# Rearranged banks, gate steps and waits, and no full-array fillers in the main part of the self-attention

## The chip, the cores and the metric

One core of a Trainium2 chip runs the whole program. The time is the device time of one launch in microseconds; the median of several runs counts. TensorE multiplies (PE in the rows, its weight loads are PEld), VectorE is DVE, ScalarE is ACT, GpSimd is POOL, and SyncE (SP) issues the transfers.

## What is computed

A pre-norm decoder layer over x of 4 batches x 512 tokens x 128 features, in fp32: causal self-attention with one head, cross-attention with 16 heads to 154 context rows, a bidirectional self-attention with 16 heads and rotary positions, and a mixture of 8 experts with the two best of each token. The reference, cut and in its own names, with h(x) a LayerNorm:

```python
a = softmax(where(causal, (x@Wq)@(x@Wk).T / sqrt(128), -inf)) @ (x@Wv)      # front
o = softmax(where(mask == 0, -inf, q@k.T * scale)) @ v ; o @ wo + bo          # cross, 16 heads of 8
attn = softmax(rope(q)@rope(k).T / sqrt(HD)) @ v ; ao @ Wo + bo              # self, 16 heads of 8
gate_probs = softmax(x1 @ Wg + bg)
topk_p, topk_i = top_k(gate_probs, 2) ; topk_p /= sum(topk_p)
h = gelu(x1 @ W1 + b1) ; y = h @ W2 + b2                                      # 8 experts, 128 -> 512 -> 128
out = layernorm(x1 + sum_e comb[e] * y[e])
```

## The kernel before

The program is written by hand for each engine; every wait is on a counting semaphore, and each engine works through its own list in order. A batch n goes through `cross(n)`, `self_attention(n)` and `tail(n)`. TensorE writes into eight banks of 128x512 fp32.

*Experts.* The 32 chunks of a batch's experts (8 experts x 4 chunks of 128 hidden features; `up` makes the hidden rows, a gelu on ScalarE, `down` adds into bank 7) are spread over the gaps of the next batch, in an order written out in `MOE_GAPS`: so many chunks at each label, "x1" to "xq" in the cross-attention's scores, "w0" to "w6" after its sums, "ta" to "tf" in the tail. No chunk stands inside the self-attention. The last batch's chunks run in one piece at the end ("all"). One bank holds the hidden rows: `up(j)` waits for the gelu of chunk j-1 (`h_act`), line 1020. When an expert's four chunks are done, VectorE scales bank 7 by the gate weights (`scale_experts`, line 692) into `ys`, GpSimd adds that to `rT`, and the next expert's first `down` waits for the scaling.

*Gate.* VectorE finds the two best experts of each token in 16 small steps (`gate_step`, line 805 on), handed out between the row maxima of the next cross-attention (`GATE_STEPS`, line 858). Its step 3 waits for GpSimd's power e**(logit - max) (`gate_exp`, line 450), and GpSimd does the rstd of the finished batch's last LayerNorm before it. TensorE writes score banks ahead of VectorE's maxima, three pairs of banks at most.

*Cross-attention* (`cross`). Scores, row maxima on VectorE (line 867), then a second pass that computes the transposed scores with the maximum subtracted: the query stack in a bank (lines 1257, 1258: high and low parts by a selection matrix), minus the maxima (line 1263). Then exponentials, sums (lines 1273, 1275), all four groups into bank 3, each copied out to `ot` before the next; heads turned and normalised; output projection; LayerNorm `ln_rows(2)`, whose rstd is a power on GpSimd; projections and rotary positions.

*Self-attention* (`self_attention`). Four groups g of four heads. For each group and each of four blocks of 128 queries, four score matmuls `s1` (line 1345, 32 rows of the array each, so several run side by side) go to a ring of three banks, and VectorE takes their row maxima (line 936). The second pass of group g runs beside the maxima of group g+1: per step (g, c) one filler, `s2` of heads 0, 1 (line 1367), `s1`, `s2` of heads 2, 3, the value sums of the step before (`sums_of`, line 1377, 128 rows x 32 columns), `s1`. `q2` (lines 1352 to 1355) starts the next group when its maxima are done. In the last group there are no scores left, and the front of the next batch (its projections and causal scores, lines 1078 to 1094) stands there.

*Fillers.* `keep_warm(n, bank)` (line 1015) issues n matmuls of 128x128 by 128x512 whose result nobody reads. They stand three by three, or one by one beside the stacks, among the first group's scores, in the first batch wherever expert chunks would be, and one ahead of each step's `s2` in the main part:

```python
if i == 0:
    keep_warm(1, 4)
for q in range(2):
    hh = 2 * i + q
    ins = pe.matmul(bank[4 + hh], kst[blk(hh), g, c * P:(c + 1) * P], q2st[blk(hh), g, :], ...)
```

*End of a batch.* `end_rows` (lines 1168 to 1175) brings the experts' sum back to token rows: the gate weights times b2, plus `ys` of the last expert, plus `rT` of the seven before it. `end_step` is the last LayerNorm.

## Time and profile before

| | |
|---|---|
| median of 3 runs | 888.74 us (887.21 to 889.29) |
| the profiled execution | 887.32 us, span 885.5 us |
| mean granted TensorE clock | 0.961 of 2.4 GHz |
| busy: TensorE, VectorE, ScalarE, GpSimd | 791.1, 428.3, 358.9, 109.4 us |
| TensorE weight loads | 403.3 us (beside matmuls) |
| transfers | 19.94 MB, 7.1% of the 16 DMA engines' span in the main queue |

An engine's busy time is the union of its instructions; a row of TensorE's timeline that merges several instructions ends with the last one's drain, so the next row may start before it ends, and the spacing of starts is what an instruction costs there. An fp32 matmul shows as two records, one of the reduced fp32r format as one. PEclk is the granted share of 2.4 GHz: 1.00 or 0.50 (1.2 GHz), or a mean of both.

### The profile page before, as it was taken

Reading aid. Unit: us, or ns where it says so; the run is one execution under the profiler, and the core shown is the slowest. Engines: PE = TensorE matmul, PEld = TensorE weight load, DVE = VectorE, ACT = ScalarE, POOL = GpSimd, SP = SyncE. Lnnn points to the kernel's source line nnn. Section 1 sums busy time; section 2 is a strip of 40 time slices with the busy share of each in tenths; the row PEclk is TensorE's granted clock in tenths of the full one; section 3 lists DMA queues with packets and bytes.
Section 4 is the critical chain, followed back from the end, with each engine's and each line's share of the span. In section 5 each row is a group of like instructions: output and inputs, shape, how many; then the busy total and the mean of one; then the engine's idle time right before and its main releaser. Section 6 shows DMA issues by size and latency. Waiting matters only on the chain.

```text
span 885.5 us, 9314 instructions
## 1 busy us (share of the span) xinstructions
PE 791.1 (89%) x3541; PEld 403.3 (46%) x3549; DVE 428.3 (48%) x1021; ACT 358.9 (41%) x494; POOL 109.4 (12%) x84
## 2 busy tenths in 40 slices
PE   4999999997979999995998999995998999994995
PEld 2774644485533543554543444544543343441332
DVE  4473597456343685345524576444622588132002
ACT  1214147622533376640442377540342267621331
POOL 4100100012012000114002100023002100014111
PEclk9999999998999999997999999998898999996998
DMA  6600000000100000000100000000000000000110
GB/s 184 202 1 1 0 1 1 1 1 2 42 12 33 15 1 1 1 25 12 43 13 24 24 1 1 1 24 0 26 13 20 28 1 1 1 24 24 36 36 24
DMA packets 18213, 19.94 MB, mean 23 GB/s; under 512 B 1730, under 2 KB 11224, under 8 KB 18168
## 3 DMA queue, kind: packets, MB, share of 16 engines
q1 hardware_dynamic: 18168, 19.34, 7.1%
q8 instruction: 28, 0.46, 0.2%
q14 instruction: 17, 0.14, 0.1%
HBM read 18.22 MB, written 1.11 MB: 22 GB/s over the span
## 4 chain that ended last, share of the span: by engine, by line
PE 77%; DVE 9%; issue 6%; POOL 4%; ACT 2%; SPq 0%; DMA 0%; POOLq 0%; DVEq 0%; ACTq 0%
PE banks L1026 13%; PE banks L1037 11%; PE banks L1015 8%; PE banks L1377 7%; PE banks L1345 5%; PE banks L1367 3%; DVE nm L936 2%; POOL gt L450 2%; PE banks L1328 2%; PE banks L1275 2%; PE banks L1244 2%; PE banks L1273 2%; PE banks L1247 2%; PE banks L1292 1%; PE banks L1286 1%
## 5 line engine op out<-in xcount | busy, mean ns | idle before, releaser
L504 ACT ACTIVATE hT<-banks,cols 128x512 f32<-128x512 f32 x128 | 87.9, 687 | 243.4 <-PE banks L1026 243.2
L936 DVE TENSOR_REDUCE nm<-banks 128x1 fp32r<-128x512 f32 x256 | 161.3, 685 | 32.4 <-PE banks L1345 31.2
L1026 PE MATMUL banks<-x1T,w 128*128 128x512 f32 x256 | 144.8, 648 | 2.4 <-ACT hT L504 2.4
L1037 PE MATMUL banks<-hT,w 128*128 128x512 f32 x256 | 134.9, 611 | 11.0 <-DVE ys L692 11.0
L635 ACT ACTIVATE px<-banks 128x1024 f32<-128x1024 f32 x128 | 125.5, 1023 | 45.3 <-PE banks L1367 44.9
L1015 PE MATMUL banks<-sel_r,eye_r 128*128 128x512 f32 x304 | 101.6, 433 | 1.0 <-ACT px L635 0.9
L692 DVE TENSOR_TENSOR ys<-banks,combB 128x512 f32<-128x512 f32 x32 | 22.1, 690 | 149.5 <-PE banks L1037 149.5
L1037 PEld LDWEIGHTS banks<-hT,w 128*128 128x128 f32 x256 | 47.7, 194 | 78.3 <-issue 51.5
L417 POOL TENSOR_TENSOR rstd<-ve,misc 128x4 f32<-128x4 f32 x20 | 20.3, 1016 | 452.0 <-DVE ve L673 452.0
L1026 PEld LDWEIGHTS banks<-x1T,w 128*128 128x128 f32 x256 | 41.8, 196 | 66.1 <-ACT hT L504 58.4
L1377 PE MATMUL banks<-px,vf 128*32 128x512 f32 x512 | 69.1, 612 | 1.4 <-ACT px L635 0.7
L1015 PEld LDWEIGHTS banks<-sel_r,eye_r 128*128 128x128 f32 x304 | 55.1, 190 | 31.6 <-issue 17.2
L1345 PE MATMUL banks<-kst,qst 32*128 32x512 f32 x256 | 66.5, 470 | 0.0
L1345 PEld LDWEIGHTS banks<-kst,qst 32*128 32x128 f32 x256 | 31.6, 182 | 52.7 <-DVE nm L936 35.6
L432 POOL TENSOR_TENSOR rT<-rT,ys 128x512 f32<-128x512 f32 x24 | 31.5, 1314 | 194.5 <-DVE ys L692 194.5
L1367 PE MATMUL banks<-q2st,kst 32*128 32x512 f32 x256 | 55.6, 500 | 0.0
L867 DVE TENSOR_REDUCE nm<-banks 128x4 fp32r<-128x616 f32 x64 | 48.7, 794 | 11.6 <-PE banks L1247 11.6
L1244 PE MATMUL banks<-mb,eye_b 128*128 128x308 bf16 x128 | 31.0, 327 | 25.6 <-DVE nm L867 24.8
L591 ACT ACTIVATE px<-banks 128x1024 f32<-128x1024 f32 x32 | 31.5, 1022 | 21.9 <-PE banks L1292 21.6
L1247 PE MATMUL banks<-kbd,qst 128*128 128x308 f32 x128 | 38.6, 386 | 0.0
L895 DVE COPY ot<-banks 128x512 f32<-128x512 f32 x16 | 11.1, 692 | 54.2 <-PE banks L1275 54.2
L1367 PEld LDWEIGHTS banks<-q2st,kst 32*128 32x128 f32 x256 | 21.8, 183 | 20.0 <-issue 17.3
(230 smaller groups left out, 947.4 us busy)
## 6 DMA issues: line engine op xcount, KB each, us to landing
combB<-gate_weights SPq DMA_DIRECT2D x32, 256.0 KB, 3.0
w<-in_L_ffn_W SPq DMA_DIRECT2D x1, 2048.0 KB, 9.5
msk<-in_mask SPq DMA_DIRECT2D x4, 308.0 KB, 4.0
xin<-in_x SPq DMA_DIRECT2D x4, 256.0 KB, 4.2
ot<-in_const_sel SPq DMA_DIRECT2D x1, 1024.0 KB
out<-outb SPq DMA_DIRECT2D x4, 256.0 KB, 2.3
cos<-in_const_cos SPq DMA_DIRECT2D x1, 256.0 KB
sin<-in_const_sin SPq DMA_DIRECT2D x1, 256.0 KB
```

Of the source, the lines that this page charges most:

```text
L504: act.activation(hT[:, j % 2, :], bank[H_BANK], ACT.Gelu, bias=cols[:, ROW_B1 + j:ROW_B1 + j + 1]).then_inc(k["h_act"], 1)
L635: act.activation(px[:, c % 2, 2 * i:2 * i + 2, :], banks[:, 4 + 2 * i:6 + 2 * i, :], ACT.Exp, scale=SCALE_H).then_inc(k["f_exp"], 1)
L867: dve.tensor_reduce(nm[:, t, g, :].rearrange("p (b h c) -> p b h c", b=2, h=2)[:, :, :, 0], banks[:, a:a + 2, 0:2 * KC].rearrange("p b (h ...
L936: dve.tensor_reduce(nm[:, t, g, BLK * hh:BLK * hh + 1], bank[s1_bank(g, t, hh)], AX.X, ALU.max, negate=True).then_inc(k["f_max"], 1)
L1015: pe.matmul(bank[i], eye_r[:], sel_r[:, 0].rearrange("p g q -> p (g q)"), start=True, stop=True)
L1026: pe.matmul(bank[H_BANK], w1[:, e, c * P:(c + 1) * P], x1T[:, p % 2, :], start=True, stop=True).then_inc(k["h_ready"], 1)
L1037: pe.matmul(bank[Y_BANK], w2[:, FC * e + c, :], hT[:, j % 2, :], start=(c == 0), stop=(c == FC - 1)).then_inc(k["y_part"], 1)
L1244: pe.matmul(bank[i][:, 0:2 * KC], eye_b[:], mb[:, t, :].unsqueeze(1).to_broadcast([P, 2, KC]), start=True, stop=False, skip_group_check=True)
L1247: ins = pe.matmul(bank[i][:, 0:2 * KC], qst[:, g, t * P:(t + 1) * P], kbd[:, g, 2 * h:2 * h + 2, :], start=False, stop=True, skip_group_ch ...
L1345: pe.matmul(bank[s1_bank(g, t, hh)], qst[blk(hh), g, t * P:(t + 1) * P], kst[blk(hh), g, :], start=True, stop=True).then_inc(k["f_s1"], 1)
L1367: ins = pe.matmul(bank[4 + hh], kst[blk(hh), g, c * P:(c + 1) * P], q2st[blk(hh), g, :], start=True, stop=True)
L1377: ins = pe.matmul(bank[3][blk(hh), :], vf[:, c, HG * g + hh, :], px[:, c % 2, hh, :], start=(c == 0), stop=(c == T - 1), skip_group_check= ...
```

## The change

What the diff does, part by part:

- A second bank (5) for the hidden rows from chunk 4 of a batch on; `up(j)` then waits for gelu j-2 only. To free bank 5 in the gaps, the uses of banks 0 to 5 in `tail`, `cross` and the first stacks are renumbered, with waits for the former users.
- The gate compares logits, not probabilities. The power takes the difference of the two best (4 values a partition instead of 32), at step 8, and its result is used at step 12. At the end of the program GpSimd does this power ahead of the second last batch's rstd, and VectorE does steps 1 to 8 ahead of that batch's moments.
- After the cross-attention the scaling of gap "w3" stands ahead of `ln_rows(2)`.
- The last group's sum of the cross-attention goes to bank 0 and waits for no copy.
- `q2` and its sibling in the cross-attention take the query stack from `qst` by one matmul with the identity.
- `end_rows` of batches 0 to 2 takes all eight experts from `rT` (GpSimd adds the eighth too) and drops the four matmuls over `ys`.
- `turn_heads` of blocks 2 and 3 both stand behind `a_sums`.
- The filler ahead of `s2` is issued only in the last group of the last batch. All other fillers stay.

```diff
@@ -105,7 +105,8 @@
-H_BANK, Y_BANK = 6, 7
+H_BANKS, Y_BANK = (6, 5), 7
+SINGLE_BANK = 4
@@ -115,7 +116,7 @@
-ST_BANKS = (4, 5, 6, 7, 4, 5, 6, 7)
+ST_BANKS = (3, 4, 5, 6, 7, 4, 5, 6)
@@ -147,6 +148,11 @@
+
+
+def h_bank(j):
+
+    return H_BANKS[0] if j < SINGLE_BANK else H_BANKS[j % 2]
@@ -307,8 +313,10 @@
-        XQ_BANKS = (0, 1, 4, 5)
+        XQ_BANKS = (1, 2, 4, 5)
...
+        X_SUM_BANKS = (3, 3, 3, 0)
+        X_HEAD_BANKS = (4, 1, 2, 3)
@@ -428,7 +436,7 @@
-                        pool.wait_ge(k["rT_added"], (NE - 1) * p + e)
+                        pool.wait_ge(k["rT_added"], NE * p + e)
@@ -447,7 +455,7 @@
-                pool.tensor_tensor(gt[:, 1], euler[:], gt[:, 0], ALU.pow).then_inc(k["g_exp"], 1)
+                pool.tensor_tensor(gs[:, 6, :], euler[:], gs[:, 5, :], ALU.pow).then_inc(k["g_exp"], 1)
@@ -483,8 +491,8 @@
                 tail(n)
+            gate_exp(B - 1)
             rstd_of(4, B - 2)
-            gate_exp(B - 1)
             end(B - 2)
@@ -685,10 +693,8 @@
                     dve.wait_ge(k["comb_loaded"], 16 * (NE * p + e + 1))
-                    if e:
-                        dve.wait_ge(k["rT_added"], (NE - 1) * p + e)
-                    elif p:
-                        dve.wait_ge(k["r_turned"], p)
+                    if p or e:
+                        dve.wait_ge(k["rT_added"], NE * p + e)
                     dve.tensor_tensor(ys[:], bank[Y_BANK], combB[:], ALU.mult).then_inc(k["y_scaled"], 1)
@@ -732,8 +738,7 @@
                     normalise_heads(0, p, 1, 4)
-                    normalise_heads(1, p, 1, 5)
-                    normalise_heads(2, p, 1, 3)
+                    normalise_heads(1, p, 1, 3)
                 if ahead:
@@ -742,7 +747,8 @@
-                    normalise_heads(3, p, 1, 4)
+                    normalise_heads(2, p, 1, 4)
+                    normalise_heads(3, p, 1, 3)
@@ -808,40 +814,40 @@
-                    own.inc(dve.reduce_max(gs[:, 0, :], flat(2), AX.X))
+                    own.inc(dve.reduce_max(gs[:, 1, :], flat(2), AX.X))
...
-                    dve.tensor_tensor(flat(0), flat(2), per_token(0), ALU.subtract).then_inc(k["g_shift"], 1)
+                    own.inc(dve.tensor_tensor(flat(3), flat(2), per_token(1), ALU.is_equal))
...
+                    own.inc(dve.tensor_tensor(flat(5), flat(3), rank, ALU.mult))
+                elif i == 4:
+                    own.inc(dve.reduce_max(gs[:, 2, :], flat(5), AX.X))
+                elif i == 5:
+                    own.inc(dve.tensor_tensor(flat(4), flat(5), per_token(2), ALU.is_equal))
+                elif i == 6:
+                    own.inc(dve.scalar_tensor_tensor(flat(8), flat(4), NEG, flat(2), ALU.mult, ALU.add))
+                elif i == 7:
+                    own.inc(dve.reduce_max(gs[:, 3, :], flat(8), AX.X))
+                elif i == 8:
+                    dve.tensor_tensor(gs[:, 5, :], gs[:, 3, :], gs[:, 1, :], ALU.subtract).then_inc(k["g_shift"], 1)
+                    own.inc(dve.tensor_tensor(flat(6), flat(8), per_token(3), ALU.is_equal))
+                elif i == 9:
+                    own.inc(dve.tensor_tensor(flat(9), flat(6), rank, ALU.mult))
+                elif i == 10:
+                    own.inc(dve.reduce_max(gs[:, 4, :], flat(9), AX.X))
+                elif i == 11:
+                    own.inc(dve.tensor_tensor(flat(7), flat(9), per_token(4), ALU.is_equal))
+                elif i == 12:
...
-                    own.inc(dve.reduce_max(gs[:, 1, :], flat(1), AX.X))
-                elif i == 4:
-                    own.inc(dve.tensor_tensor(flat(3), flat(1), per_token(1), ALU.is_equal))
-                elif i == 5:
-                    own.inc(dve.tensor_tensor(flat(5), flat(3), rank, ALU.mult))
-                elif i == 6:
-                    own.inc(dve.reduce_max(gs[:, 2, :], flat(5), AX.X))
-                elif i == 7:
-                    own.inc(dve.tensor_tensor(flat(4), flat(5), per_token(2), ALU.is_equal))
-                elif i == 8:
-                    own.inc(dve.scalar_tensor_tensor(flat(8), flat(4), -4.0, flat(1), ALU.mult, ALU.add))
-                elif i == 9:
-                    own.inc(dve.reduce_max(gs[:, 3, :], flat(8), AX.X))
-                elif i == 10:
-                    own.inc(dve.tensor_tensor(flat(6), flat(8), per_token(3), ALU.is_equal))
-                elif i == 11:
-                    own.inc(dve.tensor_tensor(flat(9), flat(6), rank, ALU.mult))
-                elif i == 12:
-                    own.inc(dve.reduce_max(gs[:, 4, :], flat(9), AX.X))
+                    own.inc(dve.tensor_scalar(gs[:, 0, :], gs[:, 6, :], 1.0, None, ALU.add))
...
-                    own.inc(dve.tensor_tensor(flat(7), flat(9), per_token(4), ALU.is_equal))
+                    own.inc(dve.reciprocal(gs[:, 7, :], gs[:, 0, :]))
...
-                    own.inc(dve.tensor_tensor(flat(2), flat(4), flat(7), ALU.add))
-                    own.inc(dve.tensor_tensor(gs[:, 5, :], gs[:, 1, :], gs[:, 3, :], ALU.add))
+                    own.inc(dve.tensor_tensor(gs[:, 8, :], gs[:, 6, :], gs[:, 7, :], ALU.mult))
+                    own.inc(dve.tensor_tensor(flat(0), flat(4), per_token(7), ALU.mult))
...
-                    own.inc(dve.tensor_tensor(flat(3), flat(2), flat(1), ALU.mult))
-                    own.inc(dve.reciprocal(gs[:, 6, :], gs[:, 5, :]))
+                    own.inc(dve.tensor_tensor(flat(1), flat(7), per_token(8), ALU.mult))
...
-                    dve.tensor_tensor(comb[:], flat(3), per_token(6), ALU.mult).then_inc(k["g_comb"], 1)
+                    dve.tensor_tensor(comb[:], flat(0), flat(1), ALU.add).then_inc(k["g_comb"], 1)
@@ -855,7 +861,7 @@
-            GATE_STEPS = ((1, 2), (3,), (4,), (5, 6), (7,), (8, 9), (10,), (11, 12), (13, 14), (15, 16))
+            GATE_STEPS = ((1,), (2, 3), (4, 5), (6,), (7, 8), (9, 10), (11,), (12, 13), (14,), (15, 16))
@@ -892,30 +898,30 @@
-                    dve.tensor_copy(ot[:, g, :], bank[3]).then_inc(k["x_ot"], 1)
+                    dve.tensor_copy(ot[:, g, :], bank[X_SUM_BANKS[g]]).then_inc(k["x_ot"], 1)
...
-                    normalise_heads(t, n, 0, (4, 5, 0, 1)[t])
+                    normalise_heads(t, n, 0, X_HEAD_BANKS[t])
...
-                own.inc(dve.tensor_tensor(x2[:].rearrange("p t d -> p (t d)"), bank[3],
+                own.inc(dve.tensor_tensor(x2[:].rearrange("p t d -> p (t d)"), bank[4],
...
+                scale_experts(p, "w3")
...
-                scale_experts(p, "w3")
...
-                    dve.scalar_tensor_tensor(rope_t[:, 2 * i, :], bank[2 * i], cols[:, ROW_FBQ + i:ROW_FBQ + i + 1],
+                    dve.scalar_tensor_tensor(rope_t[:, 2 * i, :], bank[1 + 2 * i], cols[:, ROW_FBQ + i:ROW_FBQ + i + 1],
...
-                    dve.scalar_tensor_tensor(rope_t[:, 2 * i + 1, :], bank[2 * i + 1], cols[:, COL_FBQR + i:COL_FBQR + i + 1],
+                    dve.scalar_tensor_tensor(rope_t[:, 2 * i + 1, :], bank[2 + 2 * i], cols[:, COL_FBQR + i:COL_FBQR + i + 1],
@@ -988,11 +994,11 @@
-            gate_step(B - 1, 1)
-            gate_step(B - 1, 2)
+            for i in range(1, 9):
+                gate_step(B - 1, i)
...
-            for i in range(3, 17):
+            for i in range(9, 17):
@@ -1017,13 +1023,13 @@
-                    pe.wait_ge(k["h_act"], NJ * p + j)
+                    pe.wait_ge(k["h_act"], NJ * p + (j if j <= SINGLE_BANK else j - 1))
...
-                pe.matmul(bank[H_BANK], w1[:, e, c * P:(c + 1) * P], x1T[:, p % 2, :], start=True,
+                pe.matmul(bank[h_bank(j)], w1[:, e, c * P:(c + 1) * P], x1T[:, p % 2, :], start=True,
@@ -1133,15 +1139,16 @@
+                pe.wait_ge(k["a_done"], n + 1)
+                pe.wait_ge(k["mT_ready"], 2 * (n + 1))
...
-                    dst = bank[4 + g // 2][:, (g % 2) * KC:(g % 2 + 1) * KC]
+                    dst = bank[1 + g // 2][:, (g % 2) * KC:(g % 2 + 1) * KC]
...
-                pe.wait_ge(k["x_v"], (1 + HG) * (n + 1))
@@ -1163,17 +1170,27 @@
-                pe.wait_ge(k["y_scaled"], NE * (p + 1))
-                for t in range(T):
-                    pe.matmul(bank[Y_BANK][:, t * P:(t + 1) * P], combT[:, t * P:(t + 1) * P], b2[:], start=(t == 0),
-                              stop=False, skip_group_check=True)
-                for t in range(T):
-                    pe.matmul(bank[Y_BANK][:, t * P:(t + 1) * P], ys[:, t * P:(t + 1) * P], eye[:], start=False,
-                              stop=False, skip_group_check=True)
-                pe.wait_ge(k["rT_added"], (NE - 1) * (p + 1))
-                for t in range(T):
-                    ins = pe.matmul(bank[Y_BANK][:, t * P:(t + 1) * P], rT[:, t * P:(t + 1) * P], eye[:], start=False,
-                                    stop=True, skip_group_check=True)
+                tokens = lambda t: slice(t * P, (t + 1) * P)
+                if p < B - 1:
+                    pe.wait_ge(k["rT_added"], NE * (p + 1))
+                    for t in range(T):
+                        pe.matmul(bank[Y_BANK][:, tokens(t)], rT[:, tokens(t)], eye[:], start=(t == 0),
+                                  stop=False, skip_group_check=True)
+                    for t in range(T):
+                        ins = pe.matmul(bank[Y_BANK][:, tokens(t)], combT[:, tokens(t)], b2[:], start=False,
+                                        stop=True, skip_group_check=True)
+                else:
+                    pe.wait_ge(k["y_scaled"], NE * (p + 1))
+                    for t in range(T):
+                        pe.matmul(bank[Y_BANK][:, tokens(t)], combT[:, tokens(t)], b2[:], start=(t == 0),
+                                  stop=False, skip_group_check=True)
+                    for t in range(T):
+                        pe.matmul(bank[Y_BANK][:, tokens(t)], ys[:, tokens(t)], eye[:], start=False,
+                                  stop=False, skip_group_check=True)
+                    pe.wait_ge(k["rT_added"], NE * (p + 1) - 1)
+                    for t in range(T):
+                        ins = pe.matmul(bank[Y_BANK][:, tokens(t)], rT[:, tokens(t)], eye[:], start=False,
+                                        stop=True, skip_group_check=True)
@@ -1188,17 +1205,18 @@
-                    turn_heads(1, 5)
-                    turn_heads(2, 3)
+                    turn_heads(1, 3)
...
-                    turn_heads(3, 4)
+                    turn_heads(2, 4)
+                    pe.wait_ge(k["on_ready"], T * (2 * p + 1) + 2)
+                    turn_heads(3, 3)
...
-                    pe.wait_ge(k["on_ready"], T * (2 * p + 1) + 2)
-                    turn_normalised(p, 1, 5)
+                    pe.wait_ge(k["on_ready"], T * (2 * p + 1) + 3)
+                    turn_normalised(p, 1, 4)
@@ -1209,12 +1227,12 @@
-                    turn_rows(1, n, hat1, 1)
+                    turn_rows(1, n, hat1, 4)
...
-                    pe.wait_ge(k["mT_ready"], 2 * (n + 1))
-                    pe.matmul(bank[2], wx[:, 0, :], hatT[:], start=True, stop=True).then_inc(k["x_qproj"], 1)
+                    pe.wait_ge(k["x_v"], (1 + HG) * (n + 1))
+                    pe.matmul(bank[0], wx[:, 0, :], hatT[:], start=True, stop=True).then_inc(k["x_qproj"], 1)
@@ -1253,9 +1271,7 @@
-                    dst = bank[XQ2_BANKS[g]]
-                    pe.matmul(dst, sel_r[:, 0, g, :], qhi[:], start=True, stop=False, skip_group_check=True)
-                    pe.matmul(dst, sel_r[:, 1, g, :], qlo[:], start=False, stop=False, skip_group_check=True)
+                    pe.matmul(bank[XQ2_BANKS[g]], eye_r[:], qst[:, g, :], start=True, stop=False, skip_group_check=True)
@@ -1267,12 +1283,13 @@
-                    if g:
+                    acc = bank[X_SUM_BANKS[g]]
+                    if 0 < g < G - 1:
...
-                        pe.matmul(bank[3][blk(hh), :], vx[:, HG * g + hh, :], px[:, g % 2, hh, :], start=True,
+                        pe.matmul(acc[blk(hh), :], vx[:, HG * g + hh, :], px[:, g % 2, hh, :], start=True,
...
-                    pe.matmul(bank[3], vxt[:, g, :], pxt[:, g % 2, :], start=False, stop=True,
+                    pe.matmul(acc, vxt[:, g, :], pxt[:, g % 2, :], start=False, stop=True,
@@ -1349,8 +1366,7 @@
-                    pe.matmul(dst, sel_r[:, 0, g, :], qhi[:], start=True, stop=False, skip_group_check=True)
-                    pe.matmul(dst, sel_r[:, 1, g, :], qlo[:], start=False, stop=False, skip_group_check=True)
+                    pe.matmul(dst, eye_r[:], qst[:, g, :], start=True, stop=False, skip_group_check=True)
@@ -1360,7 +1376,7 @@
-                    if i == 0:
+                    if i == 0 and g == G - 1 and b == B - 1:
@@ -1385,9 +1401,8 @@
-                            if t == 1 and i == 0 and b:
+                            if t == 2 and i == 0 and b:
...
-                                pe.wait_ge(k["h_act"], NJ * (b - 1) + FC * EXPERTS_BEFORE_F)
@@ -1401,7 +1416,7 @@
-                pe.wait_ge(k["f_st"], (2 * G - 1) * b + 5)
+                pe.wait_ge(k["f_st"], (2 * G - 1) * b + 6)
```

## Rows read from the trace of the kernel before

**Rows 1.** The page, chain that ended last: share of the span by engine.
```profile
PE 77%; DVE 9%; issue 6%; POOL 4%; ACT 2%; SPq 0%; DMA 0%; POOLq 0%; DVEq 0%; ACTq 0%
```

**Rows 2.** Waits: who waited for whom; us in total, times, longest.
```profile
DVE gs L816 <- POOL gt L450: 22.5, 4, 7.0
PE banks L1161 <- DVE comb L844: 13.6, 1, 13.6
PE banks L1037 <- DVE ys L692: 11.0, 3, 3.7
```

**Rows 3.** Timeline, gate: start us, us, instruction, idle before and releaser.
```profile
406.43 1.02 POOL L417 TENSOR_TENSOR rstd<-ve,misc 128x4 f32<-128x4 f32 x1 [16.55 <-DVE ve L673]
...
407.42 5.43 POOL L450 TENSOR_TENSOR gt<-euler,gt 128x32 f32<-128x32 f32 x1
...
804.49 0.19 DVE L816 TENSOR_REDUCE gs<-gt 128x4 f32<-128x32 f32 x1 [4.04 <-POOL gt L450]
```

**Rows 4.** Timeline, TensorE and VectorE, output part of the third batch's cross-attention.
```profile
463.63 1.02 PE L1026 MATMUL banks<-x1T,w 128*128 128x512 f32 x2
...
464.49 1.02 PE L1037 MATMUL banks<-hT,w 128*128 128x512 f32 x2
...
467.53 2.05 DVE L679 TENSOR_SCALAR hat<-x,mean,rstd 128x128 f32<-128x128 f32 x4 [1.13 <-POOL rstd L417]
469.50 0.68 DVE L692 TENSOR_TENSOR ys<-banks,combB 128x512 f32<-128x512 f32 x1
470.23 1.17 PE L1037 MATMUL banks<-hT,w 128*128 128x512 f32 x2 [3.67 <-DVE ys L692]
...
476.33 0.60 PE L1055 MATMUL banks<-eye,hat 128*128 128x128 f32 x4
```

**Rows 5.** Timeline, TensorE, the closing run of experts.
```profile
816.60 1.13 PE L1026 MATMUL banks<-x1T,w 128*128 128x512 f32 x2
...
817.56 1.02 PE L1037 MATMUL banks<-hT,w 128*128 128x512 f32 x2
...
818.50 1.13 PE L1026 MATMUL banks<-x1T,w 128*128 128x512 f32 x2
```

**Rows 6.** Timeline, TensorE: end rows, and the last sum of a cross-attention.
```profile
400.19 1.16 PE L1171 MATMUL banks<-eye,ys 128*128 128x128 f32 x8
...
451.54 1.06 PE L1273 MATMUL banks<-px,vx 128*32 128x512 f32 x8 [0.88 <-DVE ot L895]
```

**Rows 7.** Timeline, second group of the third batch's self-attention, TensorE and VectorE.
```profile
529.19 0.50 PE L1367 MATMUL banks<-q2st,kst 32*128 32x512 f32 x2
...
529.62 1.06 PE L1377 MATMUL banks<-px,vf 128*32 128x512 f32 x8
...
530.61 0.50 PE L1345 MATMUL banks<-kst,qst 32*128 32x512 f32 x2
...
531.04 0.50 PE L1015 MATMUL banks<-sel_r,eye_r 128*128 128x512 f32 x1
531.14 2.48 DVE L936 TENSOR_REDUCE nm<-banks 128x1 fp32r<-128x512 f32 x4 [0.22 <-PE banks L1345]
...
531.89 0.50 PE L1367 MATMUL banks<-q2st,kst 32*128 32x512 f32 x2
```

**Rows 8.** Timeline, TensorE, the stacks of the second pass.
```profile
523.06 0.39 PE L1353 MATMUL banks<-qlo,sel_r 128*128 128x512 f32 x1
523.29 0.56 PE L1355 MATMUL banks<-eye_r,nm 128*128 128x128 f32 x4
```

**Rows 9.** Stretches: us, busy (instructions) of PE, PEld, DVE, ACT, POOL, PEclk, DMA.
```profile
341.85:361.77 19.92, 19.23 (x108) 7.75 (x109) 6.83 (x15) 12.34 (x20) 0.00 (x0) 0.91 0.00 1
546.40:564.95 18.55, 17.85 (x108) 7.54 (x109) 6.83 (x15) 12.29 (x20) 0.00 (x0) 1.00 0.00 0
...
341.50:344.90 3.40, 2.79 (x17) 1.61 (x19) 1.79 (x4) 1.94 (x3) 0.00 (x0) 1.00 0.00 0
344.90:348.30 3.40, 3.40 (x17) 0.78 (x13) 0.00 (x0) 1.26 (x3) 0.00 (x0) 0.50 0.00 0
```

**Rows 10.** Timeline, TensorE, at the low clock.
```profile
344.73 1.84 PE L1377 MATMUL banks<-px,vf 128*32 128x512 f32 x8
...
346.50 0.80 PE L1015 MATMUL banks<-sel_r,eye_r 128*128 128x512 f32 x1
```

36 lines of the change are left out of this document (18 added, 18 removed).

## Prediction

> **What bounds the kernel now.** I read the chain of waits first: TensorE carries 77% of it [rows 1]. So a microsecond counts where TensorE runs without a gap, or where TensorE itself stands. The table of waits then gives the stops that lie on that chain. VectorE waits 22.5 us in four pieces for GpSimd's exponential of the gate, TensorE waits 13.6 us once for the last batch's gate weights, and 11.0 us in three pieces for the scaled expert output [rows 2]. The timeline shows why: the gate's power over 32 elements takes 5.43 us on GpSimd and stands behind a rstd of 1.02 us [rows 3], and in the output part TensorE stands 3.67 us for the scaling, which VectorE does behind the four normalised rows (467.53, 2.05 us), which wait for a rstd [rows 4]. In the self-attention the question is another one: is it TensorE that is full, filler included, or a loop through VectorE beside which the filler lies [rows 7]? Last comes the granted clock by stretch [rows 9].
>
> **The change, part by part.** The sum is made against the profiled execution's own 887.3 us (span 885.5), which lies 1.4 us under the median of the runs.
>
> Gate. The power moves from step 2 to step 8 and works on 4 elements a partition instead of 32, so it should cost about what a rstd of 128x4 costs, 1.02 instead of 5.43 us [rows 3]. Its result is asked for four steps later (step 12), with two row maxima between; I cost it at nothing, its cover being those maxima. If that cover were too short, about 1 us a batch would come back. The steps stay 18 small operations. The fourth of the four stops is the one in the end phase, 4.0 us [rows 3], so the three cross-attentions lose 22.5 - 4.0 = 18.5 us of VectorE stop, and TensorE stands behind VectorE there. TensorE comes out of the two longer stops at the low clock; I add half a microsecond: **19**. In the end phase the order also puts eight gate steps and the small power ahead of the LayerNorm's rows. Of the 13.6 us wait [rows 2] the 4.0 go, and part of the wait for the rstd is covered: **4.3** (4.0 to 5.5).
>
> Scaling ahead of the rows. From the first expert matmul after the output projection to the transposes of the rows are 476.33 - 463.63 = 12.70 us [rows 4]. In it stand four chunks, 8 matmuls of 0.86 us (464.49 - 463.63, the spacing where nothing waits [rows 4]), so 6.9 us. The scaling no longer waits for the rstd (1.02 us [rows 3]) and for the four rows (2.05 us); TensorE then waits about 1.0 us instead of 3.67. The rows are ready before TensorE asks. New length 7.9, gain 4.8, three times: **14.4** (3 x 2.7 = 8 if only the wait shrinks). Nothing new queues behind the scaling but the rows themselves, 0.7 us later, under four chunks of matmuls.
>
> Two hidden banks. An up and a down matmul take 1.90 us a chunk now (818.50 - 816.60 [rows 5]), since the up waits for the gelu of the chunk before. With the second bank the up needs no gelu, and a chunk takes 2 x 0.86 = 1.72. The down that opens an expert still waits for the scaled output, so three chunks of four gain 0.19. In the closing run of 28 chunks past the single-bank ones that is 21 x 0.19 = 4.0. In the gaps about 9 chunks of a batch follow one another: 27 x 0.19 = 5.1, less where another engine ends the stage, 4.5. Together **8.5** (5 to 11).
>
> Small parts. The query stacks of the second pass take one matmul instead of two, 0.23 us [rows 8]: 4 x 4 in the cross-attention are 3.7; in the self-attention 16, of which those behind the first maxima give part of it to the wait for one more stack copy: 3.4. The last sum of the cross-attention no longer waits 0.88 us for a copy out of its bank [rows 6]: 3.5. The rows of the finished batch lose the eight records over ys, about 1.0 us of the 1.16 shown [rows 6], in two batches; in the third they wait for GpSimd's last addition instead (1.3 us of work against 1.0 saved), so 0: 2.0. Sum **12.6**. The moved head transposes, the renumbered banks and the other new waits are for things long done; 0, up to 0.5 us each if a copy is late.
>
> Fillers. In the steady part one step is 2.70 us (531.89 - 529.19). Follow the loop: the second-pass pair starts at 529.19 together with the last score matmul before it, the value sums at 529.62, the next score pair at 530.61; VectorE begins its four maxima at 531.14 (2.48 us, 0.62 each), and when the first is done and its bank free, the next score matmul and second-pass pair start, 531.89 [rows 7]. 0.43 + 0.99 + 0.53 + 0.75 = 2.70: the loop closes without the filler, which stands at 531.04 beside VectorE's first maximum. So its 0.43 us (the mode change, as from 529.19 to 529.62) are worth **0** in the 36 steps that have maxima beside them (upper end: VectorE's gap of 0.22 in each [rows 7], 8 us). In the fourth group the maxima are over and TensorE does the next batch's front: there up to 4 x 0.43 a batch in three batches; the exponentials end part of it, so 1.3 each: **3.8**.
>
> Sum: 19 + 4.3 + 14.4 + 8.5 + 12.6 + 3.8 = 62.6 us of gain, 824.7.
>
> Now the clock. The filler does a second thing: it is work. In the second batch the granted clock fell from 2.4 to 1.2 GHz at 344.9 although the fillers are there; in the 3.40 us before, TensorE was busy 2.79, so it stood 0.61 in all [rows 9]. The other batches went through the same place at the full clock. The margin is thin with fillers and thinner without. One fall costs what that batch lost against the next: 19.92 - 18.55 = 1.37 us [rows 9]. I take one or two falls a batch, five more than now: **-7** (0 to -16). 824.7 + 7 = 831.7; forecast **832 us**.
>
> The Trainium skill, "TensorE: Matmul & The Clock Gate", states under "HAM oscillation" that gaps between matmuls must be long for the clock to drop; by that nothing falls here and the result would be 825. Its next section, "A second HAM failure mode: psum-queue depth-cycling", says that short micro-idles between groups of matmuls are enough to make the clock oscillate. The fall at 344.9 with no long gap before it [rows 9] speaks for the second, and what it would do here is rival 2. "TensorEngine Tiling (Array Packing)", "Key Properties", has it that a change of tiling mode drains the array; a lone filler's 0.43 us against 0.23 for one in a row [rows 7, 8] agrees, and a TensorE that was the bound would gain that much a step.
>
> **Rivals.**
> 1. *The fillers were on the path.* If VectorE's gap of 0.22 us is TensorE's doing, 36 steps gain 8 us more: 824. For it: TensorE is without a gap in the steady part. Against it: the loop closes without the filler, though the two paths lie within some 0.1 us of each other. Chance 0.15.
> 2. *The clock falls and is slow to return.* At 1.2 GHz a value-sum group takes 346.50 - 344.73 = 1.77 us instead of 0.99, and a lone filler lasts 0.80 instead of 0.50 [rows 7, 10]; a step becomes about 4.0 instead of 2.7, 1.3 more. If the low clock holds a good third of the 48 steps, 16 x 1.3 = 21, and as much again in the front matmuls and transitions: 865. For it: at half the clock the same work fills more of the time, which speaks for a quick return, but each return can be followed by a fall. Chance 0.17.
> 3. *Slower than before*, by the same mechanism when it decides: low through the whole self-attention, 12 steps x 1.3 = 16, the front and the transitions some 12, the first pass some 8, so 36 us a batch and about 140 in four: 965 in full, and over 889 once the low clock holds over 62.6/140 = 45% of the self-attention. Chance 0.04; when it falls at all, the fp32 front work of each batch should bring it back.
> 4. *The stop only moves:* VectorE waits for the small power, or GpSimd's additions come late. 3 to 5 us in all, inside the forecast's range; no case of its own.
>
> **How the numbers follow.** Forecast 0.61 (822 to 845), fillers on the path 0.15 (816 to 826), slow return 0.17 (845 to 885), slower 0.04, something I have not seen 0.03. Range 816 to 858: it holds the first two and a third of the third. A measurement of this kernel tells 0.2%, some 2 us, from no change. Faster by over that 0.95, within 0.01, slower 0.04.
>
> **What would show it.** The gate's power near 1.0 us, no stop of VectorE before its sum, and cross-attentions of the last three batches shorter by 5 to 8 us each. No 3.7 us wait of TensorE for ys, and 4.8 us less between the two points of [rows 4]. A chunk of the closing run at 1.72, 1.90 at each expert's start. Steps of the self-attention still at 2.70 with VectorE's gap still there; if they are at 2.5, rival 1. Granted clock: a handful of short falls between the groups; long stretches at 1.2 GHz would be rival 2 or 3. I am wrong if the steps lengthen at the full clock, or if the stops mended on one engine come back as waits on another.

## The result, and the profile after

| | before | after |
|---|---|---|
| median of 4 runs | 889.01 us (887.21 to 889.38) | 865.50 us (854.96 to 867.45) |
| the profiled execution | 887.32 us, span 885.5 us | 867.45 us, span 865.6 us |
| mean granted TensorE clock | 0.961 | 0.910 |

Ratio 0.972 (0.964 to 0.980): 23.5 us faster, where the forecast said 57. The executions of the changed kernel lie 12.5 us apart and those of the kernel before 2.2. Below, medians and ranges are of all executions of a kernel, since that spread is part of what is explained, and ratios only of those within 1.5% of its fastest.

The page of the changed kernel, the chain that ended last, and the granted clock in 40 slices of the span:

```profile
PE 80%; DVE 13%; issue 3%; ACT 2%; POOL 1%; SPq 0%; DMA 0%; POOLq 0%; DVEq 0%; ACTq 0%
...
PEclk9899999999999986998999955998999965895998
```

GpSimd's 4% of the chain [rows 1] are down to 1%. The clock has three dips of two or more slices with a 5 or 6 in them; the first, at the slices 15 and 16, begins at 317.5 us.

The waits that answer to [rows 2] (who waited for whom; total us, times, longest):

```profile
PE banks L1168 <- DVE comb L850: 9.6, 1, 9.6
...
PE banks L1043 <- DVE ys L698: 2.1, 3, 0.7
```

VectorE's wait for the gate's power, 22.5 us before, has no row any more, and the waits for the scaled output are 2.1 instead of 11.0 us. The stops were mended. So where did the 33.5 us over the forecast's 832 go? The main part of the self-attention, from the first value sums to the last, as stretches (length, busy time with instruction counts of PE, PEld, DVE, ACT, POOL, then PEclk), four batches of the kernel before:

```profile
127.94:175.21 47.27, 46.19 (x281) 19.15 (x282) 29.86 (x52) 32.60 (x41) 0.00 (x0) 1.00 0.00 1
312.51:361.18 48.67, 47.60 (x283) 19.36 (x282) 29.85 (x52) 32.92 (x41) 0.00 (x0) 0.96 0.01 1
517.09:564.36 47.27, 46.19 (x283) 19.15 (x282) 29.85 (x52) 32.86 (x41) 0.00 (x0) 1.00 0.00 1
721.99:765.33 43.34, 41.49 (x255) 16.02 (x254) 24.79 (x40) 32.37 (x37) 0.00 (x0) 1.00 0.00 1
```

and of the changed kernel:

```profile
128.14:173.87 45.73, 39.63 (x265) 14.91 (x265) 29.87 (x52) 33.06 (x41) 0.00 (x0) 1.00 0.00 1
298.17:352.05 53.88, 48.19 (x265) 16.58 (x265) 29.61 (x52) 33.75 (x41) 0.00 (x0) 0.78 0.00 1
491.86:552.91 61.05, 55.97 (x265) 18.56 (x265) 29.61 (x52) 34.10 (x41) 0.00 (x0) 0.64 0.00 1
692.95:750.10 57.15, 51.20 (x241) 15.95 (x241) 24.45 (x40) 33.34 (x37) 0.00 (x0) 0.64 0.00 1
```

The first batch keeps the full clock and is 1.54 us shorter than before. The other three have mean clocks of 0.78, 0.64 and 0.64, so 24, 44 and 41 us at 1.2 GHz (twice what is missing to 1, times the length). Against 45.7 us at the full clock they lose 8.2 and 15.3. The last batch has no front behind it and would take 42.2 at the full clock by an estimate (42.3 and 42.6 in two runs below, with fillers), so it loses 15.0. Together: **38.4 us**. Without the falls this execution would have taken some 829.

What the fall looks like, third batch, first the stretches on either side of it, then of the rise:

```profile
495.10:498.50 3.40, 2.78 (x19) 1.45 (x13) 3.16 (x6) 1.72 (x3) 0.00 (x0) 0.98 0.00 0
498.50:501.90 3.40, 3.40 (x15) 0.71 (x13) 0.35 (x1) 1.74 (x3) 0.00 (x0) 0.50 0.00 0
...
505.30:508.70 3.40, 3.05 (x16) 0.58 (x12) 2.48 (x4) 2.37 (x3) 0.00 (x0) 0.50 0.00 0
...
539.40:542.80 3.40, 3.40 (x20) 1.07 (x16) 0.69 (x1) 2.29 (x3) 0.00 (x0) 0.51 0.00 0
542.80:546.20 3.40, 3.40 (x22) 1.08 (x24) 1.14 (x3) 1.96 (x3) 0.00 (x0) 1.00 0.02 5
```

No long wait stands ahead of the fall; TensorE was busy 2.78 of 3.40 us, its longest wait 0.43. Once the clock is low, TensorE is busier than that, 3.05 to 3.40 us of each 3.40 but for one piece with a wait of 1.47 at the end of group 3, and yet the clock stays low for 44 us. It rises at 542.75, in group 4, where no scores are left and TensorE has no wait for VectorE's maxima:

```profile
534.34 0.77 PE L1369 MATMUL banks<-qst,eye_r 128*128 128x512 f32 x1 [1.47 <-DVE nm L942]
...
540.96 1.12 PE L1061 MATMUL banks<-eye,hat 128*128 128x128 f32 x4
...
542.74 1.06 PE L1393 MATMUL banks<-px,vf 128*32 128x512 f32 x8
543.73 1.98 PE L1084 MATMUL banks<-hatT,wa 128*128 128x512 f32 x4
```

Of the next batch's front, only four small transposes (L1061) stand ahead of the rise; its projections come 1 us after. In the last batch, which has no front, the clock rises at 740.73, in group 4 too, behind the first of the fillers that stayed there.

A step at the full clock (first batch) and a step at the low one (third batch), TensorE and VectorE:

```profile
149.54 0.50 PE L1383 MATMUL banks<-q2st,kst 32*128 32x512 f32 x2
149.97 1.07 PE L1393 MATMUL banks<-px,vf 128*32 128x512 f32 x8
...
150.97 0.50 PE L1362 MATMUL banks<-kst,qst 32*128 32x512 f32 x2
...
151.50 2.48 DVE L942 TENSOR_REDUCE nm<-banks 128x1 fp32r<-128x512 f32 x4 [0.23 <-PE banks L1362]
...
152.25 0.50 PE L1362 MATMUL banks<-kst,qst 32*128 32x512 f32 x1 [0.43 <-DVE nm L942]
...
521.15 0.79 PE L1383 MATMUL banks<-q2st,kst 32*128 32x512 f32 x2
521.87 1.94 PE L1393 MATMUL banks<-px,vf 128*32 128x512 f32 x8
...
525.31 0.79 PE L1362 MATMUL banks<-kst,qst 32*128 32x512 f32 x1 [0.35 <-DVE nm L942]
```

At the full clock a step is 152.25 - 149.54 = 2.71 us without its filler, 2.70 with it [rows 7]: the filler's place is now a wait of 0.43 for VectorE. At the low clock it is 525.31 - 521.15 = 4.16.

### The profile page after: what moved, and what is told of

Read it like the earlier page. It is cut to its first block, busy times and chain, and to the rows that moved or that the text cites. A ratio compares the mean times of both kernels' runs of the same rounds, so it can differ in the third digit from the quotient of the medians.

```text
span 865.6 us, 9085 instructions
## 1 busy us (share of the span) xinstructions
PE 785.1 (91%) x3425; PEld 393.3 (45%) x3433; DVE 432.0 (50%) x1021; ACT 363.0 (42%) x494; POOL 95.5 (11%) x87
## 4 chain that ended last, share of the span: by engine, by line
PE 80%; DVE 13%; issue 3%; ACT 2%; POOL 1%; SPq 0%; DMA 0%; POOLq 0%; DVEq 0%; ACTq 0%
PE banks L1032 12%; PE banks L1043 12%; PE banks L1393 10%; PE banks L1362 7%; PE banks L1021 6%; DVE nm L942 5%; PE banks L1383 2%; PE banks L1345 2%; PE banks L1292 2%; PE banks L1290 2%; PE banks L1262 2%; PE banks L1066 2%; PE banks L1265 2%; PE banks L1309 1%; DVE nm L873 1%
## 5 line engine op out<-in xcount | busy, mean ns | idle before, releaser
L1032 PE MATMUL banks<-x1T,w 128*128 128x512 f32 x256 | 135.4, 611 | 0.8 <-ACT hT L512 0.8
L1362 PE MATMUL banks<-kst,qst 32*128 32x512 f32 x256 | 88.8, 557 | 14.8 <-DVE nm L942 14.8
L1393 PE MATMUL banks<-px,vf 128*32 128x512 f32 x512 | 89.8, 782 | 1.4 <-ACT px L643 0.7
L1362 PEld LDWEIGHTS banks<-kst,qst 32*128 32x128 f32 x256 | 35.5, 214 | 101.5 <-DVE nm L942 84.9
L1043 PEld LDWEIGHTS banks<-hT,w 128*128 128x128 f32 x256 | 46.8, 191 | 71.6 <-issue 49.4
L1383 PE MATMUL banks<-q2st,kst 32*128 32x512 f32 x256 | 70.6, 607 | 2.1 <-ACT px L643 1.2
L1021 PE MATMUL banks<-sel_r,eye_r 128*128 128x512 f32 x244 | 71.7, 417 | 0.1
L1032 PEld LDWEIGHTS banks<-x1T,w 128*128 128x128 f32 x256 | 46.8, 195 | 44.4 <-issue 39.1
L440 POOL TENSOR_TENSOR rT<-rT,ys 128x512 f32<-128x512 f32 x27 | 35.4, 1311 | 215.3 <-DVE ys L698 215.3
L873 DVE TENSOR_REDUCE nm<-banks 128x4 fp32r<-128x616 f32 x64 | 48.6, 794 | 10.1 <-PE banks L1265 10.1
L1021 PEld LDWEIGHTS banks<-sel_r,eye_r 128*128 128x128 f32 x244 | 44.0, 191 | 17.1 <-issue 7.0
L1383 PEld LDWEIGHTS banks<-q2st,kst 32*128 32x128 f32 x256 | 26.1, 219 | 17.0 <-issue 7.6
```

The costliest lines, as they stand in the source:

```text
L873: dve.tensor_reduce(nm[:, t, g, :].rearrange("p (b h c) -> p b h c", b=2, h=2)[:, :, :, 0], banks[:, a:a + 2, 0:2 * KC].rearrange("p b (h ...
L1021: pe.matmul(bank[i], eye_r[:], sel_r[:, 0].rearrange("p g q -> p (g q)"), start=True, stop=True)
L1032: pe.matmul(bank[h_bank(j)], w1[:, e, c * P:(c + 1) * P], x1T[:, p % 2, :], start=True, stop=True).then_inc(k["h_ready"], 1)
L1043: pe.matmul(bank[Y_BANK], w2[:, FC * e + c, :], hT[:, j % 2, :], start=(c == 0), stop=(c == FC - 1)).then_inc(k["y_part"], 1)
L1362: pe.matmul(bank[s1_bank(g, t, hh)], qst[blk(hh), g, t * P:(t + 1) * P], kst[blk(hh), g, :], start=True, stop=True).then_inc(k["f_s1"], 1)
L1393: ins = pe.matmul(bank[3][blk(hh), :], vf[:, c, HG * g + hh, :], px[:, c % 2, hh, :], start=(c == 0), stop=(c == T - 1), skip_group_check= ...
```

## The experiments

"Three groups" below means one filler a step in groups 1 to 3 of each batch and in group 4 of the last batch.

**Mended stops alone.** In the changed kernel:

```diff
-                    if i == 0 and g == G - 1 and b == B - 1:
+                    if i == 0:
                         keep_warm(1, 4)
```

> The changed kernel with the full-array filler back in every step of the self-attention, so the mended stops alone. In the changed kernel the stretches outside the self-attention loop lost 51.2 us against the kernel before, and the loop of the first batch, at the full clock all through, lost 1.6; the loops of the other three gained 5.2, 13.8 and 13.8 us, with TensorE at 1.2 GHz in most of them. Theory A (the missing fillers let the clock fall): with fillers the loops are back at 12.3 us a group of four steps, 0.2 under before for the shorter query stack, and the kernel takes 887.3 - 51.2 - 2.4 = 833.7, say 829 to 838. Theory B (the mended stops themselves, one matmul instead of two in the query stacks, let the clock fall, fillers or not): low stretches of 24 to 44 us stay in batches 2 to 4, 855 to 868.

838.21 us (832.88 to 844.66), ratio to before 0.942 (0.935 to 0.950), at the upper end of theory A's range. Its four loops (the main parts of the self-attention) took 46.6, 50.7, 46.6 and 44.1 us, with 10.2 us at 1.2 GHz in the second and 3.4 in the last. That is theory A in the main. But the kernel before, with its fillers in the same places, has 3.4 us in all, and six of its seven executions beside these lie within 2.5 us of each other. That the mended stops add some falls of their own, a part of theory B, is not ruled out.

**Fillers taken out, nothing mended.** The opposite edit in the kernel before.

> The kernel before with its fillers taken out of the self-attention loop except in the last group of the last batch, nothing mended. Theory A: the loops of the last three batches go to some 54 to 61 us as in the changed kernel, 37.4 us more than they would take at the full clock, against 0.9 us a batch that the last group gains: 889 + 34 = 923 (905 to 930). Theory B: the clock falls only with the mended stops, so this one is 885 to 889. A third, that falls depend on where the self-attention starts: some batches low and others not, 895 to 915.

907.44 us (907.07 to 921.46), ratio 1.020 (1.016 to 1.025). In the profiled execution (921.46) the loops of the first and third batch took 59.6 and 65.3 us and those of the others 47.5 and 44.4. So the missing fillers cost 18 us by themselves in the median, half of what I expected, and in that execution the first batch fell. Some loops low and others not, at 907 us, is also what the third expectation had. In the first batch the clock came back at 167.24, in the third group, where neither a filler nor a front matmul stands.

**Three groups.** `if i == 0 and (g < G - 1 or b == B - 1)`.

> The mended stops with the filler in groups 1 to 3 of every batch and in group 4 of the last batch alone. Theory A: the first batch showed group 4 and the end of group 3 0.9 us shorter without fillers at the full clock; the next batch's front matmuls are full-array work of their own there. So 833.7 - 3 x 0.9 = 831, 827 to 836, and no low stretch longer than 7 us in the loop. If the filler in group 4 is needed too, a low stretch begins in group 4 of some batch and the time is 835 to 845.

835.00 us (827.16 to 838.97), ratio 0.938 (0.931 to 0.945). Three loops at the full clock, 45.7, 45.7 and (last batch) 42.6; the third 54.3, with one low stretch of 24 us. So one filler a step makes a fall rarer but doesn't rule it out, and it doesn't end one at once either: the 24 us passed with a filler in each step. The time is not told apart from that of the run with fillers in every group.

**A filler of 32 rows,** in the same places:

```diff
-                        keep_warm(1, 4)
+                        pe.matmul(bank[4], kst[blk(0), g, 0:P], qst[blk(0), g, :], start=True, stop=True)
```

> As the run with fillers in three groups, but each filler is a matmul of the kind of the scores: 32 rows of the array, 128 columns, 512 columns of data in f32, which takes TensorE as long (0.43 us). Theory A1 (what counts is that the whole array works, not that TensorE is busy): the clock falls as without fillers, 860 to 872. Theory A2 (any work in the gap counts): as with full-array fillers, 827 to 838.

864.33 us (860.47 to 871.36), ratio 0.973 (0.967 to 0.979): no help, loops of 59.9, 59.9, 53.8 and 42.3 us. But the traces show that such a filler runs beside the scores. One group at the full clock, first with the 32-row filler, then with one full-array filler a step:

```profile
510.00:522.32 12.32, 10.87 (x77) 4.19 (x73) 9.74 (x17) 9.46 (x12) 0.00 (x0) 1.00 0.00 0
```

```profile
128.98:141.27 12.29, 11.87 (x73) 4.92 (x73) 9.77 (x17) 8.52 (x11) 0.00 (x0) 1.00 0.00 1
```

TensorE is busy 10.87 us against 11.87, so this run alone doesn't say whether the array or the time was missing. Three later runs take that up.

**Every other step,** of the three groups (`c % 2 == 0`).

> As the run with fillers in three groups (835.0 us), but in every other step only. Theory A (full-array work is what holds the clock, and each filler adds to it): the clock is lost in some of the batches, for a part of the loop, 843 to 858, between 835 with a filler in each step and 865 with none. If one filler in two steps suffices: 827 to 839. If one in two is as good as none: 860 to 870.

848.42 us (845.13 to 853.79), ratio 0.955 (0.951 to 0.959): half the fillers, half the gain.

**Two a step,** `keep_warm(2, 4)`, three groups.

> As the run with fillers in three groups, but two in a row in each step. The run with one a step still had one low stretch of 24 us in the third batch's loop, worth 54.3 - 45.7 = 8.6 us. Theory A: with twice the full-array work no long low stretch is left in any loop, and the second filler, without a change of mode, costs 0.2 us at most where it has no cover: loops of 45.7 to 48, kernel 825 to 834, and the spread of its runs smaller. Rival: the second filler stands on the path, 12 steps x 4 x 0.21 = 10 us: groups of 13.1 instead of 12.3, kernel 836 to 845.

831.18 us (829.78 to 832.27), ratio 0.935 (0.933 to 0.937). The loops took 46.0, 46.0, 46.0 and 43.5 us and the spread is down to 2.5 us. A group:

```profile
313.24:325.68 12.44, 12.30 (x81) 4.93 (x85) 10.31 (x16) 8.83 (x11) 0.00 (x0) 1.00 0.01 1
```

12.44 instead of 12.30: the second filler costs 0.14 us a group, not the 0.84 of the rival, and no loop has a fall. Against the undisturbed loops with one filler a step, these are 0.3 us longer, the last one 0.9, and the stretch from a batch's first scores to its first value sums is 0.24 longer, some 2.8 us in all. The fastest execution with one a step, 827.16 us, is below all of these.

**The changed kernel, 2 us later.** `keep_warm(10, 6)` ahead of the first tail.

> The changed kernel as it is, with ten full-array matmuls (2.1 us) put ahead of everything that follows the set-up, so that all later work comes some 2 us later. In the changed kernel the first batch's loop stayed at the full clock and the other three fell, with the same work in each. Theory C (without fillers each loop stands at the edge, and whether it falls, and where, is a matter of when it starts): other batches or other points of the loops fall, loops of 46 to 62 us in another pattern, 855 to 875. Rival (the first batch stays up because of something in it, such as its missing expert chunks): the same three batches fall in the same groups, and the first stays at 45.7.

860.48 us, from 841.07 to 885.39. In the profiled execution the loops took 48.1, 46.6, 52.8 and 56.7 us, where they took 45.7, 53.9, 61.1 and 57.2 before the shift. All four had a fall, of 6.8, 3.4, 20.5 and 41.0 us. The rival, that something in the first batch protects it, falls. The third one ended, at 529.21, ahead of the first front matmul (L1061), in the middle of a row of value sums, which take 1.94 us at the low clock and 1.06 at the full one:

```profile
526.23 1.94 PE L1393 MATMUL banks<-px,vf 128*32 128x512 f32 x8
...
528.83 1.23 PE L1393 MATMUL banks<-px,vf 128*32 128x512 f32 x8
529.99 0.66 PE L1061 MATMUL banks<-eye,hat 128*128 128x128 f32 x4
```

So the front's full-array work isn't needed for the rise. That the moment of the start alone decides isn't shown, since the executions of this one program differ by 44 us.

**Is it time or the array?** Two 32-row fillers ahead of each step's second-pass scores; then a third ahead of the other pair; then one filler a step from the same buffers on all 128 rows (`kst[:, g, 0:P]`, `qst[:, g, :]`).

> The changed kernel with two fillers of 32 rows in a row ahead of each step's second-pass scores (groups 1 to 3, and group 4 of the last batch). One such filler gave 864.3 us and TensorE busy 10.87 of 12.32 us in a group at the full clock. With two I expect 11.5 to 12.3 busy. If time in which TensorE works is what the missing fillers took away: 828 to 845. If it is work of the whole array: low stretches of 20 to 45 us in at least two of the four loops, 855 to 880.

838.61 us (837.10 to 854.88); TensorE busy 11.65 of 12.30 us in a group; loops 49.4, 46.9, 45.7 and 48.3. The time is in the range of the theory that counts time, though two loops had a low stretch of 10 and 17 us.

> As the run before it with a third filler of 32 rows, ahead of the step's other pair of second-pass scores. TensorE should have no idle time left, 12.3 of 12.5 us or more in a group as with two full-array fillers (831.2 us); the third stands on the path for 0.2 to 0.4 us a step, up to 15 us in the kernel. If time is what counts: no long low stretch, 832 to 848. If the whole array's work is: low stretches as without fillers, 865 to 900.

889.68 us (856.96 to 897.07). A group at the full clock, and the stretch ahead of a fall in the second batch:

```profile
300.90:314.12 13.22, 12.64 (x81) 5.36 (x81) 9.99 (x17) 9.80 (x11) 0.00 (x0) 1.00 0.00 1
...
317.70:321.10 3.40, 3.12 (x23) 1.80 (x16) 2.95 (x5) 1.70 (x3) 0.00 (x0) 1.00 0.00 0
321.10:324.50 3.40, 3.40 (x16) 1.03 (x15) 0.06 (x2) 1.48 (x2) 0.00 (x0) 0.51 0.02 5
```

> As the run with one filler of 32 rows a step, with the same operands on all 128 rows: one two-pass matmul of 128x128 by 128x512, 0.43 us at the full clock and some 0.4 more for the two changes of mode around it. Either theory expects the clock held: 827 to 840; if it stands on the path with 0.2 us a step, groups of 13.1 and 836 to 845. At 855 or more neither theory would be right, and it would be the reduced format of the fillers that matters.

839.02 us (832.97 to 842.87), with the pattern of the three-groups run: 45.7, 45.7, 54.4 and 42.7. The expectation calls its filler a two-pass matmul, but the buffers `kst` and `qst` hold the reduced format, and it is one record a step in the trace, as the other fillers are:

```profile
133.57 0.49 PE L1380 MATMUL banks<-qst,kst 128*128 128x512 f32 x1
```

With three small fillers TensorE is busy 12.64 of 13.22 us, about the share that one full-array filler a step gives (11.87 of 12.29). The longer steps explain some 0.92 x 3 x 4 = 11 us over the 831 without falls, and the executions lie 15 to 55 us above that, against 0 to 12 for the one full-array filler over its lowest. So filling TensorE's time isn't enough. All fillers, small and large, are of the reduced format, so it doesn't tell them apart; whether it matters, no run shows. Two small fillers did better than three, which neither theory expected.

How long the clock was at 1.2 GHz within the four loops, one trace a kernel:

| fillers ahead of `s2` | us at 1.2 GHz |
|---|---|
| none | 109 (changed kernel), 72 (2 us later), 99 (kernel before) |
| a full-array one in every other step of three groups | 72 |
| a full-array one a step | 3.4 (kernel before) and 14 (changed kernel), in every group; 24, 24 and 14, in three groups |
| two full-array ones a step | 0 in all five traces |
| 32 rows: one, two, three a step | 106, 30, 51 |

That full-array fillers keep the clock up, and two a step better than one, is shown. Whether they do it because the whole array works or because TensorE has fewer pauses stays open: two small ones did nearly as well as one large one, three did worse.

**The terms of the sum, one at a time.** Both on the version with two fillers a step, whose clock is steady. The rows ahead of the scaling again:

```diff
-                scale_experts(p, "w3")
                 ln_rows(2, n, x2, hat3, k["ln_hat2"])
+                scale_experts(p, "w3")
```

> As the run with two fillers a step (831.2 us), but VectorE again does the four normalised rows ahead of the scaling in the output part, as in the kernel before: this sizes one term of the forecast by itself. The forecast had 4.8 us a batch for it, 14.4 in three, from 12.70 us to 7.9 between the two points of the output part; the changed kernel's trace has 7.85 there. If the term was right: 845.6 (844 to 847) and output parts of 45.6 instead of 40.8 us. If only TensorE's wait counts (3.67 against 0.71): 840.1.

844.69 us (843.32 to 846.28): 13.5 more than 831.18. From the last value sums of a cross-attention to the first scores of the self-attention are 45.65 us against 40.81.

One hidden bank, `SINGLE_BANK = 32`:

> As the run with two fillers a step (831.2 us), but with one hidden bank for all 32 chunks. The forecast gave the second bank 8.5 us (5 to 11): 4.0 in the closing run and 4.5 in the gaps. In the changed kernel an expert of the closing run takes 7.06 instead of 7.61 us, 0.55 x 7 = 3.9, as forecast. If the gaps' share was right too: 839.7. If the gaps give nothing, since other engines end those stages: 835.1.

840.36 us (839.61 to 841.93): 9.2 more. Those output parts are 0.94 longer each, and two tails 1.74.

**The last gate first.** On the three groups:

```diff
-            end_step(B - 2, 0)
-            for i in range(1, 9):
+            for i in range(1, 17):
                 gate_step(B - 1, i)
-            end_step(B - 2, 1)
-            end_step(B - 2, 2)
-            for i in range(9, 17):
-                gate_step(B - 1, i)
+            for i in range(3):
+                end_step(B - 2, i)
```

> As the run with fillers in three groups, but in the end phase VectorE does all of the last gate's steps ahead of the finished batch's LayerNorm. In the changed kernel VectorE stands 4.96 us for that batch's rows from TensorE with the gate's sixteen steps queued behind, and TensorE then 9.6 us for the weights. The steps and the small power take some 5 us, which fit into that wait; the weights come some 9 us earlier. What is late next is the first down matmul, which waits for the normalised rows: they end some 3.5 us earlier, since the gate no longer stands in between. Forecast: 4 to 7 us less than 835.0, so 830 (824 to 834); 0 if the rows' own path (POOL's rstd, the four rows) is what ends.

826.59 us (823.53 to 838.84), ratio 0.929 (0.925 to 0.933), more than I expected, though one of its four executions is as slow as the slowest with the three groups alone. The gap between the last gate's logits and the turn of its weights is 747.67 - 741.68 = 5.99 us instead of 15.70, so 9.7 less (the next expectation has 8.0):

```profile
741.68 0.95 PE L1159 MATMUL banks<-wg,x1T 128*128 128x8 f32 x8
743.97 1.67 PE L1174 MATMUL banks<-eye,rT 128*128 128x128 f32 x8 [1.33 <-POOL rT L440]
...
747.67 1.01 PE L1165 MATMUL banks<-eye,comb 128*8 128x128 f32 x4
...
751.17 2.08 PE L1029 MATMUL banks<-x1T,w 128*128 128x512 f32 x2 [0.78 <-ACT hT L512]
```

**Both together,** two fillers a step and the gate first:

> Two fillers a step and the last gate ahead of the finished batch's rows. Two fillers a step gave 831.2 with little spread; the gate first moved the last batch's comb turn 8.0 us nearer to the gate logits and the kernel 8.4 us down. If they add: 822 to 825, with a spread of 3 us instead of 15. If one low stretch in the loops comes back: 827.

822.31 us (821.26 to 823.95), ratio 0.925 (0.924 to 0.926). They add: against two fillers a step alone it is 8.9 us less, and the ranges are 5.8 us apart.

**And fillers in the end phase:**

> As the run before it, with full-array fillers in the two places of the end phase where TensorE stands: six ahead of the finished batch's rows (1.33 us of wait) and eight ahead of the first down matmul. There the clock falls in each run, for 10 to 20 us, and the first three expert matmuls take 1.7 us instead of 0.86 each. If the fillers hold the clock: 2 to 4 us less than the run before. If the clock falls all the same, because the gate's and the rows' small matmuls on either side do too little: 0 to 1 us more than the run before.

822.02 us (821.82 to 822.11), ratio 0.924 (0.923 to 0.926): the same within what can be told. The stretch at 1.2 GHz after the logits is 3.4 us long instead of 6.8, but the first down comes 752.14 - 739.81 = 12.33 us after them instead of 750.93 - 740.13 = 10.80, behind the eight fillers. These last two beat both kernels, by 67 and 43 us.

## Why the prediction was wrong

The direction was right and the sum nearly so, the clock's term was not. By the profiled executions, the changed kernel against before:

- *Gate, 18.5 of the 19:* the score parts of the last three cross-attentions are 5.60, 6.06 and 6.75 us shorter, 18.4. The power takes 1.01 us, and its two maxima cover it there. No run undid this term by itself.
- *Gate in the end phase, 4.3:* **wrong size.** From the last logits to the turn of the weights it was 809.29 - 791.65 = 17.64 and is 791.38 - 775.68 = 15.70, 1.9. I had costed the third batch's rows at 0 because 1.3 us of addition stood against 1.0 saved. The rows wait 1.33 us and then run at the low clock, and VectorE stands for them with the gate queued behind:

```profile
775.68 0.95 PE L1162 MATMUL banks<-wg,x1T 128*128 128x8 f32 x8
777.97 1.83 PE L1177 MATMUL banks<-eye,rT 128*128 128x128 f32 x8 [1.33 <-POOL rT L440]
779.73 2.07 PE L1180 MATMUL banks<-b,combT 8*128 8x128 f32 x8
791.38 1.02 PE L1168 MATMUL banks<-eye,comb 128*8 128x128 f32 x4 [9.59 <-DVE comb L850]
```

- *Scaling ahead of the rows, 14.4:* right. The two points of [rows 4] are 7.85 us apart, forecast 7.9, and the undo cost 13.5:

```profile
443.67 1.02 PE L1032 MATMUL banks<-x1T,w 128*128 128x512 f32 x2
...
447.12 1.13 PE L1043 MATMUL banks<-hT,w 128*128 128x512 f32 x2 [0.71 <-DVE ys L698]
...
451.52 0.60 PE L1061 MATMUL banks<-eye,hat 128*128 128x128 f32 x4
```

- *Two hidden banks, 8.5:* right; the undo cost 9.2. In the closing run an expert takes 811.19 - 804.13 = 7.06 us against 4 x 1.90 = 7.6 [rows 5], 3.9 in seven, of which 1.7 went to its start at the low clock (9.03 us from the turn of the weights to the fourth up matmul, where it was 7.31):

```profile
804.13 1.02 PE L1032 MATMUL banks<-x1T,w 128*128 128x512 f32 x2
...
811.19 1.02 PE L1032 MATMUL banks<-x1T,w 128*128 128x512 f32 x2
```

- *Small parts, 12.6:* nearly. Second pass and last sum of the cross-attention 7.5 (forecast 7.2). The rows of a finished batch, 2.0 forecast: the tails are 2.6 shorter in two batches, of which the second bank gave 1.7, so 1.7 in all. In the self-attention a group is 0.21 shorter by the stack, 2.5 in all instead of 3.4. The first pass is 0.1 longer a batch, and the first cross-attention began 1.86 us later, beside a fall twice as long at the start.
- *Fillers, 0 in the steps and 3.8 in group 4:* right at the full clock. The step is 2.71 us, the first batch's groups 1 and 2 lost only the stack's 0.21 each, and its groups 3 and 4 lost 0.66 and 0.47, 0.9 a batch or 2.8 in three. Rival 1 is wrong: VectorE's gap of 0.22 stayed. The 36 steps are a slip, though: four batches have 48 steps in groups 1 to 3, as rivals 2 and 3 count, so rival 1 would have been worth up to 10.6 us.
- *Clock, -7:* **this step failed.** I put five more falls at 1.37 us each, the price of the one fall in the loops of the kernel before, 3.4 us long. In the changed kernel the three falls lasted 24, 44 and 41 us, each into its batch's group 4, and cost 38.4 us, 12.8 each, nine times the price. The row I took it from [rows 9] shows one fall among fillers, and the change removes them, so it was no bound. It wasn't even a price with fillers: in the traces of the experiments a fall in the loops lasts 3.4 to 24 us with one a step and 3.4 to 55 without any. What the fillers change is how often a fall comes and how long the clock is low in sum (the table above). Low for long is the mechanism of rival 2, to which I gave 0.17.

Rival 2's 865 is the measured number, but by other terms. It had 16 steps of 1.3 us and as much again in the front matmuls and the transitions. A low step cost 4.16 - 2.71 = 1.45, some 109 / 4.16 = 26 steps were low, and the front matmuls lost next to nothing, since but for the first four they came after the rise (group 4 took 10.1 us in each of the first three batches).

Without falls the changed kernel stands at some 829 us by the estimate above, where the sum had 824.7: the terms other than the clock came out 4 us short, most of it in the end phase's gate and the small parts. The 831.2 us with two fillers a step, so near to the forecast's 831.7, is chance: it has those 4 us and the fillers' own cost in it, and no falls in the loops. Rival 3 was to decide from 45% of the self-attention at the low clock. 26 of 48 steps are 54%, and the kernel is still faster: the rival had priced 36 us a batch with the first pass and the front in it, and both ran at the full clock but for the front's first four matmuls.

The Trainium skill, "TensorE: Matmul & The Clock Gate", "HAM oscillation", has the clock drop only after a long gap between matmuls. The trace doesn't agree: the drop at 498.50 has no wait over 0.54 us in the 6 us ahead of it. Its section "A second HAM failure mode: psum-queue depth-cycling" says that frequent micro-idles between groups of matmuls make the clock oscillate. The trace agrees with the first half, with waits of 0.19 to 0.54 us there, and not with the second: in each of the three loops the clock fell once and stayed low for 24 to 44 us.
